# A decoder with six attentions: value products in 64x64 quadrants, and heads summed in the output product

## The reference

```
q, k, v = h @ Wq + bq, c @ Wk + bk, c @ Wv + bv        # c is h or the context
per head: p = softmax(mask(scale * q_h @ k_h.T));  o_h = p @ v_h
x = norm(x + concat(o_h) @ Wo + bo)
```

```
t1, t2 = split(t, 2, axis=-1);  t2 = pad(t2, one zero token ahead)[:, :-1];  h = concat(t1, t2)
```

## Time and profile before

| what | value |
|---|---|
| time, median of 3 runs | 1068.12 us (1063.12 to 1068.31) |
| the profiled execution | 1074.77 us, span 1073.0 us |
| PE busy | 869.9 us (81%), 5275 matmuls and as many loads |
| PEld busy | 659.9 us (62%) |
| DVE, ACT, POOL busy | 610.3, 541.6, 298.0 us (57%, 50%, 28%) |
| mean granted TensorE clock | 0.83 |
| chain that ended last | PE 49%, DVE 22%, ACT 10%, issue 8%, POOL 6% |

### The profile page before, as it was taken

How to read it: one execution, slowest core, us unless ns; L and a number is a source line. 1 busy time by engine, 2 the same in 40 slices (tenths; PEclk the granted TensorE clock), 3 DMA queues, 4 the chain that set the end, 5 groups by cost and what they waited for, 6 DMA issues and landing times.

```text
span 1073.0 us, 15676 instructions
## 1 busy us (share of the span) xinstructions
PE 869.9 (81%) x5275; PEld 659.9 (62%) x5275; DVE 610.3 (57%) x1568; ACT 541.6 (50%) x1292; POOL 298.0 (28%) x460
## 2 busy tenths in 40 slices
PE   5787976888887867899867999659379779799997
PEld 3465854666566746888446888425246678756765
DVE  5846738888888357868466654313138768321122
ACT  2125625578776637866346653214148467133342
POOL 4335512332334220111244432120243335200011
PEclk8756857899998968989858866669779889579999
DMA  6050000000000000000340000021624200000000
GB/s 263 1 188 29 1 1 1 1 2 1 2 1 2 1 1 1 1 1 1 109 126 2 1 1 1 5 76 35 193 99 157 60 1 1 1 1 1 1 8 13
DMA packets 29645, 37.26 MB, mean 35 GB/s; under 512 B 2688, under 2 KB 20864, under 8 KB 29056
## 3 DMA queue, kind: packets, MB, share of 16 engines
q1 hardware_dynamic: 29056, 35.21, 10.0%
q0 software_dynamic: 512, 1.05, 0.3%
HBM read 28.00 MB, written 8.26 MB: 34 GB/s over the span
## 4 chain that ended last, share of the span: by engine, by line
PE 49%; DVE 22%; ACT 10%; issue 8%; POOL 6%; DMA 1%; DVEq 0%; POOLq 0%; ACTq 0%
PE bank L650 6%; PE bank L842 6%; PE bank L852 5%; PE bank L631 5%; DVE mx L1318 3%; PE bank L641 3%; PE bank L802 3%; ACT pairs L937 2%; DVE sm L1315 2%; POOL sm L1633 2%; PE bank L659 2%; PE bank L607 2%; ACT pr L957 2%; PE bank L694 2%; PE bank L664 1%
## 5 line engine op out<-in xcount | busy, mean ns | idle before, releaser
L1604 POOL TENSOR_SCALAR veps<-mv 128x1 f32<-128x1 f32 x112 | 26.9, 240 | 396.8 <-DVE mv L1248 396.7
L1633 POOL TENSOR_TENSOR sm<-sm,mx 128x512 f32<-128x512 f32 x80 | 83.6, 1045 | 153.1 <-DVE mx L1318 152.9
L650 PEld LDWEIGHTS bank<-VX,pT 128*128 128x128 f32 x896 | 123.3, 220 | 0.3 <-issue 0.3
L650 PE MATMUL bank<-VX,pT 128*128 128x34 f32 (+1 forms) x896 | 122.3, 292 | 0.0
L937 ACT ACTIVATE pairs<-bank,bkm,quad 128x128 f32<-128x128 f32 x224 | 84.1, 456 | 28.0 <-PE bank L607 25.6
L957 ACT ACTIVATE pr<-sm 128x512 f32<-128x512 f32 x112 | 70.4, 636 | 41.2 <-POOL sm L1633 37.9
L631 PE MATMUL bank<-pairs,Q 64*128 64x256 f32 x448 | 81.1, 491 | 0.0
L963 ACT COPY pT<-bank 128x512 f32<-128x512 f32 x112 | 61.4, 592 | 31.5 <-PE bank L641 31.1
L1537 DVE SCALAR_TENSOR_TENSOR XB<-bank,QM,XB 128x128 f32<-128x128 f32 x64 | 18.0, 343 | 94.2 <-PE bank L852 94.2
L641 PE MATMUL bank<-W,pr 128*128 128x128 f32 x448 | 69.6, 307 | 0.4 <-ACT pr L957 0.4
L842 PE MATMUL bank<-XT,big 128*128 128x512 f32 x128 | 66.8, 650 | 2.4 <-ACT G L1109 2.4
(11 more groups left out here) (296 smaller groups left out, 1956.6 us busy)
## 6 DMA issues: line engine op xcount, KB each, us to landing
big<-gup SPq DMA_DIRECT2D x4, 1024.0 KB, 8.9
rel_scratch<-G SPq DMA_DIRECT2D x16, 256.0 KB, 2.9
W<-small SPq DMA_DIRECT2D x1, 3622.5 KB, 12.8
big<-early SPq DMA_DIRECT2D x2, 1557.0 KB, 8.1
big<-down SPq DMA_DIRECT2D x8, 256.0 KB, 8.8
big<-e3w SPq DMA_DIRECT2D x2, 1024.0 KB
big<-e3w SPq DMA_DIRECT2D x8, 256.0 KB
QM<-rel_scratch SPq DMA_DIRECT2D x16, 128.0 KB, 2.7
```

The source lines that it names most:

```text
L650: last = mm(ps[:, p * blk:(p + 1) * blk], pT[:, u % 2, p, :], V[:, 8 * s_ + p, :], start=True, stop=True)
L1633: tt(v, v, bc(mx[:, slot, :], [P, 8, S], 2), ALU.subtract).then_inc(pcentered, 1)
```

## The change

- The value step becomes 32 products for each unit: 64 rows (one sequence), 64 columns (the queries of one of the pair's heads), 9 moving columns (8 values and a one for the sum; in x2 5). Sequence 0 goes into bank 6 and sequence 1 into bank 7.
- DVE writes V with one operation; its reciprocals and products are two each, one for a bank, into OB, where the heads' outputs of even heads lie on one half of the partitions and of odd heads on the other.
- The fold becomes one transpose of OB. The output product is four products into bank 6: oT's even and odd halves against WO, which is the output weight with the rows of other heads and sequences set to zero.
- WO is made once for each attention (step `weights`): two products with the 0/1 matrices pick16 or pick32 into bank 7, and two ACT copies.
- The memory ON is no longer cleared between stages; more zeroing falls away at the start. DVE builds next_token, pick16 and pick32 in the start.
- In the local layers steps `hs` go; `st` multiplies X1 by the identity and by the shift matrix next_token. Banks are dealt out anew and PATIENCE is 0.05 for 0.2.
- `SHIFT` and the planned times of all other steps stay.

```
+ATT_STEPS = {"kv": 0, "weights": 1.05, "project": 0.3, ...}      # REL_STEPS: "weights": 3.0
+                    if step == "weights" and t + s_:
+                        continue
...
-HOP, OWN, RELOAD, PATIENCE = 0.2, 0.1, 1.5, 0.2
-LOCAL_BANK = {"q": (0,), "k": (1,), "tq": (2,), "tk": (3,), "sc": (4,), "v": (3,), "tp": (0,), "va": (3, 4), "out": (7,),
-              "hs": (7,), "st": (2,), "hn": (7,), "ug": (6,), "ua": (5,), "dn": (3,), "ag": (0,), "x": (7,)}
+HOP, OWN, RELOAD, PATIENCE = 0.2, 0.1, 1.5, 0.05
+LOCAL_BANK = {"q": (1,), "k": (4,), "tq": (2,), "tk": (3,), "sc": (5,), "v": (6,), "tp": (3,), "va": (2, 5), "out": (6,),
+              "st": (4,), "hn": (6,), "ug": (7,), "ua": (0,), "dn": (7,), "ag": (1,), "x": (0,)}
...
                         pe.wait_ge(v_split, at_["v", t])
                         ps = fill(6, on_ready)
+                        ps = [ps, fill(7, on_ready)]
                         for p in range(8):
-                            last = mm(ps[:, p * blk:(p + 1) * blk], pT[:, u % 2, p, :],
-                                      V[:, 8 * s_ + p, :],
-                                      start=True, stop=True)
-                        last.then_inc(valued, 1)
+                            for c in range(2):
+                                for b in range(2):
+                                    r, m = slice(b * S, (b + 1) * S), slice(c * S, (c + 1) * S)
+                                    last = mm(ps[b][m, p * blk:(p + 1) * blk], pT[r, u % 2, p, m], V[r, 16 * s_ + 2 * p + c, :],
+                                              start=True, stop=True)
+                                    if p == 7 and c == 1:
+                                        last.then_inc(valued, 1)
                         at_["on", t] = due.now(on_ready)
+                    if step == "weights":
+                        ps = fill(7, wo_ready)
+                        for c in range(2):
+                            pick = (pick16 if wide else pick32)[:, c, :, :].rearrange("p b n -> p (b n)")
+                            last = mm(ps[:, c * P:(c + 1) * P], pick, w(f"{name}.o"), start=True, stop=True)
+                        last.then_inc(wo_full, 1)
+                        at_["wo", name] = due.now(wo_ready)
                     if step == "fold":
                         pe.wait_ge(on_ready, at_["on", t])
-                        ps = fill(7, o_ready)
-                        for b in range(2):
-                            last = mm(ps[:, b * S:(b + 1) * S], spread(name, t)[:, b, :], w("fold"), start=True, stop=True)
-                        last.then_inc(folded, 1)
+                        pe.transpose(fill(7, o_ready)[:, 0:P], OB[:, t % 4, :], ident).then_inc(folded, 1)
                         at_["o", t] = due.now(o_ready)
                     if step == "residual" and a:
                         pe.wait_ge(o_ready, at_["o", t])
-                        mm(fill(7, y_used)[:, 0:P], oT[:, t % 2, :], w(f"{name}.o"), start=True, stop=True).then_inc(y_full, 1)
+                        pe.wait_ge(wo_ready, at_["wo", name])
+                        ps = fill(6, y_used)
+                        for b in range(2):
+                            for c in range(2):
+                                last = mm(ps[b * S:(b + 1) * S, 0:P], oT[:, t % 2, c * S:(c + 1) * S],
+                                          WO[:, a["i"] % 2, b, c, :], start=(c == 0), stop=(c == 1))
+                        last.then_inc(y_full, 1)
...
-                    if step == "hs":
+                    if step == "st":
                         pe.wait_ge(x1_ready, n + 1)
-                        pe.transpose(fill(b_[0], hs_ready)[:, 0:P], X1[:, t, :], ident).then_inc(shifted, 1)
...
+                        ps = fill(b_[0], hn_ready)
+                        mm(ps[:, 0:S], ident, X1[:, t, 0:S], start=True, stop=True)
+                        mm(ps[:, S:P], next_token[:, :], X1[:, t, S:P], start=True, stop=True).then_inc(restored, 1)
...
+                    if step == "weights":
+                        act.wait_ge(wo_full, due(wo_full))
+                        for b in range(2):
+                            r = slice(b * S, (b + 1) * S)
+                            last = act.copy(WO[r, a["i"] % 2, b, :, :].rearrange("p c n -> p (c n)"), bank[7][r, 0:2 * P])
+                        last.then_inc(wo_ready, 1)
...
-                        for b in range(2):
-                            r = slice(b * S, (b + 1) * S)
-                            last = tt(V[r, :, b * n:(b + 1) * n], bank[4][r, 0:P].rearrange("p (h d) -> p h d", d=n),
-                                      w(f"{name}.bv")[r].rearrange("p (h d) -> p h d", d=n), ALU.add)
-                        last.then_inc(v_split, 1)
+                        tt(V[:, :, 0:d], bank[4][:, 0:P].rearrange("p (h d) -> p h d", d=d),
+                           w(f"{name}.bv").rearrange("p (h d) -> p h d", d=d), ALU.add).then_inc(v_split, 1)
...
+                        o = [bank[6 + b][:, 0:8 * blk].rearrange("p (h n) -> p h n", h=8) for b in range(2)]
+                        for b in range(2):
+                            dve.wait_ge(valued, due(valued))
+                            last = dve.reciprocal(rs[:, u % 2, b, :], o[b][:, :, d])
+                        link(last)
+                        dst = OB[:, t % 4, :].rearrange("p (b s h d) -> p b s h d", b=2, s=2 if name == "x2" else 1, d=d)
+                        for b in range(2):
+                            tt(dst[:, b, s_, :, :], o[b][:, :, 0:d], bc(rs[:, u % 2, b, :], [P, 8, d], 2),
+                               ALU.mult).then_inc(on_ready, 1)
```

More of the change, by code:

```diff
@@ L71, in now @@
         return self.count.get(id(sem), 0)
-ATT_STEPS = {"kv": 0, "project": 0.3, "scores": 1.1, "turn": 2.5, "values": 3.7, "fold": 4.9, "residual": 5.4,
+ATT_STEPS = {"kv": 0, "weights": 1.05, "project": 0.3, "scores": 1.1, "turn": 2.5, "values": 3.7, "fold": 4.9, "residual": 5.4,
              "finish": 6.65}
-REL_STEPS = {"kv": 2.0, "project": 0.3, "rel": 1.15, "scores": 4.1, "turn": 5.5, "values": 6.7, "fold": 7.9,
+REL_STEPS = {"kv": 2.0, "weights": 3.0, "project": 0.3, "rel": 1.15, "scores": 4.1, "turn": 5.5, "values": 6.7, "fold": 7.9,
              "residual": 8.4, "finish": 9.65}
@@ L1038, in first_ffn @@
                                 "p (a q) -> p a q", q=S)).then_inc(ot_ready, 1)
-                    if step == "hs":
-                        if n >= 2:
-                            act.wait_ge(restored, n - 1)
-                        act.wait_ge(shifted, n + 1)
-                        src = bank[LOCAL_BANK["hs"][0]][:, 0:P].rearrange("p (b k) -> p b k", b=2)
-                        act.copy(HS[0:S, t % 2, :, :], src[0:S])
-                        act.copy(HS[S:P, t % 2, :, 1:S], src[S:P, :, 0:S - 1]).then_inc(hs_ready, 1)
                     if step == "hn":
@@ L1157, in rotary, with token_shift, head_picks @@
                     tt(rot[:, l, i, :], w(table), w(f"f{l}.{scale}"), ALU.mult)
+            def token_shift():
+                dve.tensor_copy(next_token[:, 1:P], w("ident", 0, P - 1))
+                link(dve.memset(next_token[:, 0:1], 0.0))
+                link(dve.memset(next_token[:, S:S + 1], 0.0))
+            def head_picks():
+                for c in range(2):
+                    for v, d in ((pick16, 8), (pick32, 4)):
+                        for b in range(2):
+                            last = dve.tensor_copy(v[:, c, b, :].rearrange("p (h d) -> p h d", d=d),
+                                                   w("ident").rearrange("p (h c d) -> p c h d", c=2, d=d)[:, c, :, :])
+                link(last)
             def fading():
@@ L1578, in _ @@
             n_init = 0
[L1579 to L1589 removed]
+            for v, number in ((VX[:, :, :, 8:9], 1.0), (VX32[:, :, :, 4:5], 1.0), (HT[:, :, 0:1], 0.0), (zero[:, :], 0.0),
+                              (WO[:, :, :, :, :], 0.0)):
+                pool.memset(v, number).then_inc(pool_init, 1)
+            pool.memset(QM[:, :, :, :, :], 0.0)
+            pool.memset(ON[:, :, :, :], 0.0).then_inc(zeroed, 1)
             pool.wait_ge(first_in, 32)
@@ L1639, in first_ffn @@
             def first_ffn():
-                pool.wait_ge(x_ready, due.now(x_ready))
-                pool.memset(ON[:, :, :, :], 0.0).then_inc(zeroed, 1)
                 for step, l, t, n in local["pool"]:
```

102 lines of the change are left out of this document (33 added, 69 removed).

## The result

The changed kernel takes 1103.54 us (median of 4 runs, 1095.96 to 1107.23), the kernel before 1068.21 us in the same comparison (1063.12 to 1072.75). The ratio is 1.032, 95% interval 1.025 to 1.040. The forecast was 1097 us.

What follows compares the result with a forecast made beforehand. At the full clock the order around DVE bounds attention units, PE's value products being cover. Loops +40, x2 +3.5, half clock -14, weights +4, clock +5, first layers -10, start +1: +29, 1097 us; range 1080 to 1115 (8 in 10: 1056 to 1130).

Steps and rivals of the forecast that it cites:

- Both waits: Attention units: value products wait for DVE's residual add (bank 6), fold for DVE's values (bank 7); 1.5 to 2 us a unit.
- The loop in x1: One unit of x1 at the full clock, both new waits inserted: 7.76 us against 6.34, +1.4.
- The sum of the loops: Attention loops, 17 x 1.4 + 8 x 1.65 + 3 = +40 us; with half clock, weight step and clock terms +35.
- the gain of 14 us there: Half-clock stretches outside x2 and units outside the loops: PE is late, so less work gains; -14 us (0 to -35).
- the +5 for the clock: PE idle twice in a unit may drop a few more stretches to 1.2 GHz: +5 us (0 to +60).
- x2: Stage folding every second unit: +0.5 us for each of 7 pairs, +3.5 us (bounds -10 and +8).
- Local layers: First layer pair, 150 to 388 us: vanished transpose and ACT copies shorten each unit's path; -10 us (-35 to +8).
- The weight step: Run six times; PE waits behind bank 7's last copy with scores queued behind: 0.4 to 1.2 us each, taken +4.
- (a): Rival: PE's smaller products win if the bank waits find DVE already done; -25, 1043 us; chance 0.18.
- (b): Rival: half-clock and first-layer gains meet the +43 of losses; 1066 to 1070 us; chance 0.10.
- (c): Rival: PE's idling puts all 28 loops at 1.2 GHz, +65 at most; half gives 1130 us; chance 0.10.
- (d): Rival: 25 ns between matmul starts makes value steps 1.8 us in loops and x2 pairs; +21, 1118 us; chance 0.06.

Runs made afterwards that it cites:

- e1: Kernel before, products kept, but with the changed kernel's banks (value step also waits for bank 7, output product into bank 6): 1215.98 us, ratio 1.136.
- e3: Changed kernel with only the fold's planned time moved earlier, 4.9 to 4.45 (a3: 7.9 to 7.45): 1046.44 us, ratio 0.977 to the kernel before.
- e9: Changed kernel with the output product in bank 4 instead of 6, planned at 5.55 for 5.4 (a3: 8.55 for 8.4): 1069.01 us, ratio 1.000.
- e6: Changed kernel with both the earlier fold (4.45) and the output product in bank 4 at 5.55: 1020.70 us, ratio 0.961 to the kernel before.
- e7: Changed kernel with each value product issued twice into the same place: 1201.99 us, ratio 1.135 to the kernel before.
- e11: Kernel before with only the local layers' token shift by matrices, old banks and PATIENCE 0.2 kept: 1067.46 us, ratio 1.000.
- e8: e6 with each value product issued twice into the same place: 1104.09 us, ratio 1.041 to the kernel before.

## Why the prediction was right, and where some of its terms were not

**The mechanism** holds. Both waits are in the trace where they were put (477.75 behind 477.14; 480.73 behind 480.23), e1 makes the loss without the small products, and e3, e9 and e6 give it back wait by wait. In the two rounds shown PE waits 0.66 + 1.05 and 1.22 + 1.05 us for DVE, where 1.5 to 2 us a unit were forecast; over the whole kernel the two entries of the list make 61 us, 1.1 a unit.

**The loop in x1** was put at 7.76 us and is 7.71 (477.14 to 484.85), 6.34 before. Its terms were off both ways: the value step 1.12 us (taken 1.16), DVE's values 0.65 (0.95; 479.93 to 480.58), from the end of the residual add to the first value product 0.33 (0.11), the output product 0.66 (0.7) in the same loop.

**The sum of the loops** was too small. For x0, a1 to x1 and a3 to x3 the forecast had 40 - 14 + 4 + 5 = +35 us; measured are 3.3 + 28.2 + 23.3 = +55. At the full clock the unit was right, so most of the 20 us probably stand at the half clock; no run separates them. The terms that failed are the gain of 14 us there and the +5 for the clock. I took the gain because PE was late and would do less. But in a loop that PE and DVE take in turns each of PE's steps is on the path, and the half clock lengthens them (scores 2.08 us for 1.13); the granted clock also fell from 0.94 to 0.81 in a1 and x1 and from 0.87 to 0.74 in a3 and x3. The score steps wholly at the half clock went from 4 to 7 of 16 in a1 and x1 and from 3 to 7 of 16 in a3 and x3: about 7 us for the scores alone, an estimate (7 x 0.95). The five last intervals of x1, which need no K and V, grew from 24.2 to 35.9 us, 2.3 each where 1.65 was taken; one of these has its scores at the half clock.

**x2** had the wrong sign: +3.5 forecast, -9.9 measured. The step that failed is the loop of two units, worked out on DVE's order at the full clock with a correction for the other. At the granted clock of 0.74 PE is busy 91.10 of 100.89 us, and less work for PE is what counts. The bound given (-10) just held it. e7 agrees: x2 grows by 18.2 us with the products doubled. The waits seem to cost something there all the same: without one or both x2 takes 7 to 9 us less (e3, e9, e6), though at higher granted clocks (0.82, 0.84 and 0.80).

**Local layers**: -10 taken, -13.4 measured in the stretch, within its bounds. The reason given was half wrong: the shorter path of a unit is worth nothing by itself (e11); the gain comes only with the new banks and PATIENCE.

**Small terms**: start, g, the experts and the tail, +1 forecast and about +1 measured together. The weight step shows no time of its own in any stage's difference that could be told from the loops, so its +4 is not settled.

So the total, +29 forecast and +32.4 measured, is better than its parts: the loops were 20 us too cheap, x2 and the local layers 17 us too dear. That the two nearly cancel is luck; the direction and the two waits are not.

**The rivals.** (a) PE's saving wins: false for the change as it stands, since DVE had not finished when PE arrived, which was the condition named; true in x2; with both waits gone the whole kernel is faster (e6), though not by PE's saving alone. (b) A draw: false. (c) The clock falls: in part. In a1 and x1 it fell from 0.94 to 0.81 and in a3 and x3 from 0.87 to 0.74, but not to the half clock throughout; x0 (0.73 and 0.74) and x2 (0.74 in both) kept theirs, and the mean of the run fell from 0.83 to 0.81. e1, with the old products, shows that the waits alone bring such a fall. (d) Small pairs slow: false. 64 loads take 1.02 to 1.05 us at the full clock, and in e8 128 take 2.02, so a further load costs 1.00 us / 64 = 15.6 ns. The Trainium skill ("TensorE: Matmul & The Clock Gate", section "Wait — 56ns, not 53.3ns?") gives about 25 ns as the least from start to start; for these 64x64 products the measurement decides against it.

## What to carry to other kernels

Before two steps share a memory bank, write down for every refill who must have read it, and where that reader stands in its own engine's order; in an in-order queue the refill holds all that is behind it. A saving on an engine counts by stage: the smaller value products made x2, where PE was full, 9.9 us shorter, and a1 with x1, where two new waits came with them, 28.2 us longer. When a change with shorter steps comes out slower, list the new waits and move one buffer and one step before giving it up: e6 differs from the slower kernel by four planned times and one bank, and is 83 us faster.

## What the runs showed of the hardware

- A 64x64 load with its product of 9 columns follows the last after 15.6 ns on average at the full clock (e8, above), 1.12 us for 64 with the tail. The starts are not even: in the step at 477.72 of the changed kernel three follow after 6 to 10 ns each and the fourth after 35 ns, throughout.
- Steps of 128 such pairs don't always run through: in e7 and e8 PE stood idle inside them with nothing to wait for, up to 2.4 us (e7), where 64 pairs show no such wait in the changed kernel or in e6. The waits of PE in e8 that end by "issue" (total, times, longest):

```profile
PE bank L655 <- issue: 14.1, 14, 1.7
```

  That is 14 of e8's 83 us, and 13.7 us in e7. The cause is open.
- The same instructions of x0 ran at a mean granted clock of 0.73 in one program and 0.87 in another, 47.0 and 40.7 us. A difference of 6 us in a stage that a change does not touch is thus no evidence about the change.
